# Second expert layer: the rank products of its second half put directly behind that half's router products, the shared expert's products put behind them, and products on zeros placed ahead of two waits

## The chip, the cores and the metric

The kernel runs on one core of one Trainium2 chip. Its time is that of one execution of the whole program in device microseconds (us), the median over several runs. TensorE (PE) has a granted clock with two levels here, 1.2 and 2.4 GHz; the profile prints it as a share of the higher one, so 0.50 is the lower level. VectorE is DVE, ScalarE is ACT, GpSimd is POOL, SyncE is SP.

## The reference

The input x has 4 batches of 256 tokens with 256 features, 1024 tokens in all. Four layers follow one another, each of the form x = x + tanh(gate) * layer(layernorm(x)): a sparse attention, an expert layer of 8 experts, a latent attention with 16 heads, and the second expert layer, in which the change lies. Cut to what matters here:

```python
    router_logits = (x @ gate_w).astype(jnp.float32)          # x: normed tokens, 1024 x 256; gate_w: 256 x 16
    scores = jax.nn.sigmoid(router_logits)
    _, selected = jax.lax.top_k(scores + expert_bias[None, :], K)      # K = 2 of E = 16 experts
    top_scores = jnp.take_along_axis(scores, selected, axis=1)
    top_scores = top_scores / (top_scores.sum(-1, keepdims=True) + 1e-20)
    shared = jax.nn.silu(x @ shared_gate_w) * (x @ shared_up_w) @ shared_down_w
    for e in range(E):
        gu = x @ experts_gate_up[e]
        g, u = jnp.split(gu, 2, axis=-1)
        routed = routed + comb[:, e:e + 1] * (jax.nn.silu(g) * u @ experts_down[e])
    return (shared + routed).reshape(b, s, h)
```

So each token has a shared expert, which needs no routing, and two of 16 experts that its router picks.

## The kernel before, in words

All tokens stay on the chip as 8 tiles of 128 tokens, worked on in two halves of 4 tiles (512 tokens). Each engine has an order of instructions of its own, written out by hand, and the engines wait for each other by semaphores. An engine works through its list strictly in that order.

The second expert layer starts when the last attention lap has been added to x. For each half (called 0 and 1, Python argument `hf`) the steps are these.

- DVE norms the tokens into `xn` (ACT norms two of half 1's four tiles, L368). PE transposes them (`pe_transpose`, L399), ACT copies the result in full precision (`plain1_act`, L544, into the tile named att_w_raw) and rounded (`act_high`, L409, xT_h), and DVE forms the rest (`low`, L415, xT_l).
- PE multiplies the router weights (`logits1_pe`, L554, 8 products of 16 columns). ACT takes the sigmoid (L561). DVE finds the two best experts per token (`choose1`, L568 to L581) and writes `chosen`, a 0/1 matrix of tokens by experts.
- PE counts, by products with a triangular matrix, how many earlier tokens picked the same expert (`rank_pe`, L591 to L599, small bf16 products into bank 2). The last of them raises the semaphore `s_rank`.
- DVE turns rank and choice into a row number, the slot (`slots`, L609 to L615), and raises `s_slot`.
- POOL writes each token's normed row into its two slots in DRAM (`Blocks.place`, L955), 8 indirect transfers (DMA_INDIRECT, destination `xn_slots`) for each half, each of one tile of 128 rows.

When all 16 transfers of both halves have landed and DVE has worked out which expert owns which block (`compact`, L621 to L627, and `owners`, L633 to L648, which raises `s_owner`), SP loads the blocks of 128 rows back (`moe_x`, L991). Then come 31 blocks, each with a transposition (L998), gate and up products (L1007), a transposition of the hidden rows (L1016) and a down product (L1023) on PE, and an indirect store to `y_rows` (L962) on POOL. At the end the two rows of a token are read back and added to x.

The shared expert runs between these steps: `ffn1.gateup` (L803) makes 12 products of 512 columns for each half: 8 with the rounded weights (`wt_h`: xT_h and xT_l, gate and up) and 4 with the weights' rest (`wt_l`). ACT applies silu (L740), DVE multiplies (L752), `pe_down_whole` (L825) makes the down products and DVE adds them to x (L776). The products of half 1 need xT_l of half 1, which DVE makes (L415) only behind `slots` of half 1.

`fill` (L1714) and `warm` (L1031) multiply zeros into a bank that nobody reads, 512 columns each. `warm` makes 15 of them when the third quarter of the scatters has landed and 8 when the fourth has; `FILLS` is 6.

## Time and profile before

| | before |
|---|---|
| median of 3 runs (lowest to highest) | 541.48 us (541.19 to 542.93) |
| the profiled execution, its own time | 542.32 us |
| its span, first to last instruction | 539.3 us |
| PE busy | 492.2 us (91%) |
| DVE busy | 413.0 us (77%) |
| mean granted PE clock over the span | 0.975 |

The profiled execution's own time is 3.0 us longer than its span: what lies around the first and the last instruction. A row of a timeline gives the start in the span, the busy time, engine, line, operation, output and inputs, shape and count, and in brackets how long the engine sat idle before it and what ended that. Durations of PE rows overlap, since products are pipelined and their ends are modelled: the pace of a series is read from starts.

### The profile page before, as it was taken

The page shows a single profiled execution, that of the slowest core. Times are in us where ns is not written, and L with a number is a line of the kernel's source. Part 1 is how long each engine was busy: PE and PEld are TensorE (multiplying, and loading weights), DVE is VectorE, ACT ScalarE, POOL GpSimd, SP SyncE. Part 2 cuts the span into 40 slices and gives each one's busy share as a digit, 9 for nine tenths or more (in the row PEclk, how much of TensorE's full clock was granted, in tenths as well). Part 3 has the DMA queues.
Part 4 walks back from the last instruction along what each step waited for, and adds up shares of the span by engine and source line. Part 5 has one row for each costly group of instructions (what it writes and reads, how often), then busy time and mean ns, then how long its engine had stood idle before and what let it go on. Part 6 is the DMA issues. An engine that isn't in the chain of part 4 may idle for free.

```text
span 539.3 us, 9166 instructions
## 1 busy us (share of the span) xinstructions
PE 492.2 (91%) x2781; PEld 380.6 (71%) x2781; DVE 413.0 (77%) x1054; ACT 310.6 (58%) x793; POOL 281.5 (52%) x291
## 2 busy tenths in 40 slices
PE   6976999989988997789999999999999977999986
PEld 3754688777867885457777777777776665778864
DVE  5998899974677759888999999999997864644322
ACT  4753654335554641377777777787776872155541
POOL 0060467657335733568787768786660026345560
PEclk9997999999999999999999999999999986999998
DMA  7596423223412319881909080816006502234416
GB/s 258 192 280 226 139 58 89 88 60 89 147 60 62 114 39 234 148 174 35 195 11 197 14 191 29 176 50 126 1 2 246 235 19 80 98 113 121 135 57 233
DMA packets 40281, 65.03 MB, mean 121 GB/s; under 512 B 4323, under 2 KB 30637, under 8 KB 39984
## 3 DMA queue, kind: packets, MB, share of 16 engines
q1 hardware_dynamic: 37984, 60.31, 40.7%
q0 software_dynamic: 2256, 4.21, 2.4%
q8 instruction: 20, 0.33, 0.3%
q14 instruction: 21, 0.17, 0.1%
HBM read 38.48 MB, written 27.99 MB: 123 GB/s over the span
## 4 chain that ended last, share of the span: by engine, by line
PE 62%; DVE 23%; issue 4%; DMA 3%; ACT 3%; POOL 2%; another core or an unknown queue 1%; SPq 1%; POOLq 0%; DVEq 0%
PE bank L1592 11%; PE bank L803 8%; PE bank L1647 5%; PE bank L1666 5%; PE bank L1636 5%; PE bank L1007 4%; PE bank L838 4%; PE bank L1609 3%; DVE left L1978 3%; PE bank L1626 3%; PE bank L1613 2%; PE bank L1627 2%; DVE best L1974 2%; PE bank L1023 2%; DVE hid L759 2%
## 5 line engine op out<-in xcount | busy, mean ns | idle before, releaser
L1424 POOL TENSOR_TENSOR qr<-qr 128x512 f32<-128x512 f32 x48 | 61.7, 1285 | 16.0 <-DVE qr L2090 16.0
L2090 DVE TENSOR_TENSOR qr<-bank,sinq 64x512 f32<-64x512 f32 x96 | 66.1, 689 | 2.2
L1825 ACT ACTIVATE silu<-bank,negm 128x256 f32<-128x256 f32 x128 | 59.3, 472 | 6.1 <-DVE negm L2104 6.0
L720 POOL TENSOR_TENSOR ffn_w_l<-ffn_raw,ffn_w_h 128x512 fp32r<-128x512 f32 x30 | 39.4, 1315 | 30.1 <-ACT ffn_w_h L732 30.0
L1429 POOL TENSOR_TENSOR hid<-silu,rden 128x256 f32<-128x256 f32 x55 | 33.8, 615 | 35.4 <-DVE rden L2109 35.3
L2104 DVE TENSOR_REDUCE negm<-bank 128x2 f32<-128x512 f32 x64 | 44.2, 691 | 6.3 <-PE bank L1627 3.7
L744 ACT ACTIVATE hid_h<-hid 128x512 fp32r<-128x512 f32 x28 | 17.7, 631 | 52.9 <-DVE hid L759 46.6
L1832 ACT ACTIVATE hid<-silu,rden 128x256 f32<-128x256 f32 x55 | 27.9, 507 | 34.2 <-DVE rden L2109 34.2
L962 POOL DMA_INDIRECT y_rows<-moe_y,route_rows x31 | 30.2, 974 | 31.1 <-issue 18.1
L1838 ACT ACTIVATE probsT<-bank 128x512 f32<-128x512 f32 x64 | 37.9, 592 | 9.8 <-PE bank L1636 9.6
L803 PE MATMUL bank<-xT_h,ffn_w_h 128*128 128x512 f32 x120 | 40.5, 419 | 2.9 <-DVE xT_l L415 2.9
L1636 PE MATMUL bank<-ident,hid 128*128 128x128 f32 x256 | 38.5, 273 | 2.4 <-POOL hid L1429 1.1
L803 PE MATMUL bank<-xT_l,ffn_w_h 128*128 128x512 f32 x120 | 39.4, 410 | 0.0
L1626 PE MATMUL bank<-ks_h,qs 128*128 128x256 f32 x128 | 34.6, 293 | 4.0 <-DVE qs L2098 2.5
L1592 PE MATMUL bank<-xT_h,att_w_h 128*128 128x512 f32 x96 | 34.5, 442 | 3.5 <-DVE xT_l L415 2.7
L803 PE MATMUL bank<-xT_h,ffn_w_l 128*128 128x512 f32 x120 | 34.1, 406 | 0.0
L2086 DVE TENSOR_TENSOR qr<-bank,cosq 128x512 f32<-128x512 f32 x48 | 32.7, 682 | 1.1 <-PE bank L1592 1.0
L1627 PE MATMUL bank<-ks_l,qs 128*128 128x256 f32 x128 | 32.8, 280 | 0.0
L740 ACT ACTIVATE silu<-bank 128x512 f32<-128x512 f32 x30 | 17.8, 593 | 26.0 <-PE bank L803 25.9
L838 PE MATMUL bank<-ffn_w_h,hid_h 128*128 128x256 f32 x112 | 28.5, 288 | 4.5 <-ACT hid_h L744 4.5
L1007 PE MATMUL bank<-moe_w,moe_xT 128*128 x124 | 32.1, 382 | 0.0
L1099 DVE COPY moe_hidT<-bank 128x128 f32<-128x128 f32 x31 | 9.0, 292 | 29.9 <-PE bank L1016 29.9
(259 smaller groups left out, 1393.2 us busy)
## 6 DMA issues: line engine op xcount, KB each, us to landing
xn_slots<-blank SPq DMA_DIRECT2D x8, 2056.0 KB, 12.9
ffn_raw<-in_w_ffn SPq DMA_DIRECT2D x30, 256.0 KB, 2.7
pair_w<-in_pair_w SPq DMA_DIRECT2D x8, 768.0 KB, 5.7
moe_w<-in_w_moe SPq DMA_DIRECT2D x1, 6144.0 KB, 18.2
moe_x<-xn_slots SPq DMA_DIRECT2D x31, 128.5 KB
ffn_raw<-in_w_ffn SPq DMA_DIRECT2D x30, 128.0 KB, 2.3
folds<-att_w_raw SPq DMA_DIRECT2D x6, 640.0 KB, 8.3
att_w_raw<-folds SPq DMA_DIRECT2D x6, 384.0 KB, 12.2
```

The lines of the kernel that those rows point to most:

```text
L720: nc.gpsimd.tensor_tensor(wt_l[b][:, 0:GU], raw[b][:, 0:GU], wt_h[b][:, 0:GU], ALU.subtract).then_inc(self.wgl, 1)
L803: last = nc.tensor.matmul(bank[self.up(st) + g][:], wp[st.b][:, (2 * kt + g) * P:(2 * kt + g + 1) * P], xp[:, kt, st.hf * 512:(st.hf + 1) ...
L838: last = nc.tensor.matmul(bank[4 + t // 2][:, (t % 2) * D:(t % 2 + 1) * D], hp[st.b][:, t * P:(t + 1) * P], wp[st.b][:, GU:WC], start=Fals ...
L1007: last = nc.tensor.matmul(bank[2 + b % 2][:, 0:2 * P], xgT[b % 2][:, k, :], cells[:, bass.ds(cell + k * 2 * P, 2 * P)], start=(k == 0), st ...
L1424: nc.gpsimd.tensor_tensor(qr[n][:, 0, :], qr[n][:, 0, :], qr[n][:, 1, :], ALU.add).then_inc(s_turned, 1)
L1592: last = nc.tensor.matmul(bank[bk][:], m_of(wp[w], k, j), xp[:, k, hf * 512:(hf + 1) * 512], start=(m == 0), stop=(m == 5))
L1626: nc.tensor.matmul(o, q, ks_h[:, keys], start=True, stop=False)
L1627: last = nc.tensor.matmul(o, q, ks_l[:, keys], start=False, stop=True)
L1636: last = nc.tensor.matmul(bank[6][:, (2 * h + k) * P:(2 * h + k + 1) * P], pn[u % 2][:, h, k * P:(k + 1) * P], ident[:], start=True, stop= ...
L1825: last = nc.scalar.activation(ex[u % 2][:, h, :], bank[4 + u % 2][:, h * S:(h + 1) * S], ACT.Exp, bias=negm[:, u % 2, h:h + 1], accum_out= ...
L2090: last = nc.vector.tensor_tensor(by_sin[other, :, :], q2[hs, :, :], sinq[hs, j:j + 1, :].broadcast_to([C, 2, S]), ALU.mult)
L2104: nc.vector.tensor_reduce(negm[:, u % 2, :], bank[4 + u % 2][:].rearrange("p (h n) -> p h n", h=2), AX_X, ALU.max, negate=True).then_inc(s ...
```

## The change

Only PE's order is touched, at one place behind the last attention lap. Eight products on zeros are put between the rank products of half 0 and the wait for half 1's normed tokens. Four more, and then the rank products of half 1, are put directly behind half 1's router products. The first half's shared expert products, which in the kernel before enclose the rank products of half 1 (8 ahead of them, 4 behind), come behind them as one series of 12. The wait on `s_slot` (half 0's ranks read from bank 2) moves with the rank products.

```diff
                 logits1_pe(pe, 0)
                 fill(FILLS, 5)
                 rank_pe(pe, 0)
+                fill(8, 5)
                 n_ffn1[1].pe_transpose(pe)
                 logits1_pe(pe, 1)
+                pe.wait_ge(s_slot, 1)
+                fill(4, 5)
+                rank_pe(pe, 1)
                 n_ffn1[0].pe_whole(pe)
-                ffn1.gateup(pe, ffn1_first, ((wt_h, (0, 1)),))
-                pe.wait_ge(s_slot, 1)
-                rank_pe(pe, 1)
-                ffn1.gateup(pe, ffn1_first, ((wt_l, (0, 1)),))
+                ffn1.gateup(pe, ffn1_first)
                 n_ffn1[1].pe_whole(pe)
                 ffn1.gateup(pe, ffn1_second)
```

On PE, from half 0's last rank products (L599) on, the rows of the change with + and those of before with - read as follows; bank<-zero is a product on zeros, ident,xn the transposition, rg_raw,att_w_raw the router products.

```order
 L599 MATMUL bank<-chosen,route_tri 128x32
 L599 MATMUL bank<-chosen,route_tri 128x16
+L1714 MATMUL bank<-zero 128x512 x8
 L399 MATMUL bank<-ident,xn 128x128 x8
 L554 MATMUL bank<-rg_raw,att_w_raw 128x16 x8
-L803 MATMUL bank<-xT_h,ffn_w_h 128x512 x2
-L803 MATMUL bank<-xT_l,ffn_w_h 128x512 x2
-L803 MATMUL bank<-xT_h,ffn_w_h 128x512 x2
-L803 MATMUL bank<-xT_l,ffn_w_h 128x512 x2
+L1714 MATMUL bank<-zero 128x512 x4
 L591 MATMUL bank<-route_expert_rows,route_tri 128x64
 L593 MATMUL bank<-chosen,route_tri 128x64
```

Eight shared expert products have left the place between the router products and the rank products, and zeros stand in two places.

Behind half 1's last rank products, the same engine goes on like this; ffn_w_h are the rounded weights of the shared expert, ffn_w_l their rest.

```order
 L599 MATMUL bank<-chosen,route_tri 128x32
 L599 MATMUL bank<-chosen,route_tri 128x16
+L803 MATMUL bank<-xT_h,ffn_w_h 128x512 x2
+L803 MATMUL bank<-xT_l,ffn_w_h 128x512 x2
+L803 MATMUL bank<-xT_h,ffn_w_h 128x512 x2
+L803 MATMUL bank<-xT_l,ffn_w_h 128x512 x2
 L803 MATMUL bank<-xT_h,ffn_w_l 128x512 x4
 L803 MATMUL bank<-xT_h,ffn_w_h 128x512 x2
```

The eight products that left stand here now, so that 12 products of the first half follow the rank products, where 4 did. The order of DVE, ACT, POOL and SP is the same in both kernels.

## Rows read from the trace of the kernel before

**Rows 1.** The page: the span.

```profile
span 539.3 us, 9166 instructions
```

**Rows 2.** The chain that ended last, 448 to 470 us: start, us, what.

```profile
448.37 4.67 another core or an unknown queue
...
463.70 3.14 DMA xn_slots<-moe_xn_second,route_slot_at
...
467.59 2.17 DMA moe_x<-xn_slots
```

**Rows 3.** Timeline of POOL, its indirect transfers.

```profile
450.76 0.98 POOL L955 DMA_INDIRECT xn_slots<-moe_xn_second,route_slot_at  x1 [0.30 <-issue]
454.74 0.97 POOL L955 DMA_INDIRECT xn_slots<-xn,route_slot_at  x1 [3.00 <-DVE route_slot_at L615]
```

**Rows 4.** Timeline of DVE: half 1's choice and slots, the owners' first and last instruction.

```profile
448.33 0.23 DVE L581 TENSOR_TENSOR chosen<-one_hots 128x64 bf16<-128x64 f32 x1
453.06 0.29 DVE L609 TENSOR_TENSOR route_smul<-one_hots,bank 128x128 f32<-128x128 f32 x1 [4.50 <-remote]
...
453.70 0.17 DVE L615 CAST route_slot_at<-route_slot 128x8 uint32<-128x8 f32 x1
...
461.00 0.15 DVE L633 TENSOR_TENSOR route_ends<-route_base,route_nblk 1x16 f32<-1x16 f32 x1
...
464.77 0.17 DVE L648 COPY route_owner<-route_row_f 1x31 f32<-1x31 f32 x1
```

**Rows 5.** Timeline of PE around the change, and its first block's transposition.

```profile
433.63 1.85 PE L554 MATMUL bank<-rg_raw,att_w_raw 128*128 128x16 f32 x16
435.33 1.63 PE L1714 MATMUL bank<-zero 128*128 128x512 f32 x6
...
441.23 1.38 PE L399 MATMUL bank<-ident,xn 128*128 128x128 f32 x8 [2.16 <-DVE xn L374]
442.66 3.57 PE L554 MATMUL bank<-rg_raw,att_w_raw 128*128 128x16 f32 x16
...
449.63 0.28 PE L591 MATMUL bank<-route_expert_rows,route_tri 128*128 128x64 bf16 x1
...
450.02 0.34 PE L599 MATMUL bank<-chosen,route_tri 128*128 128x64 bf16 x4
450.21 2.05 PE L803 MATMUL bank<-xT_h,ffn_w_l 128*128 128x512 f32 x4
455.12 0.88 PE L803 MATMUL bank<-xT_h,ffn_w_h 128*128 128x512 f32 x2 [2.86 <-DVE xT_l L415]
...
459.57 3.62 PE L825 MATMUL bank<-ffn_raw,hid 128*128 128x256 f32 x16
462.83 3.80 PE L1031 MATMUL bank<-zero 128*128 128x512 f32 x15
466.88 2.14 PE L1031 MATMUL bank<-zero 128*128 128x512 f32 x8 [0.25 <-DMA xn_slots<-moe_xn_second,route_slot_at]
469.07 0.44 PE L998 MATMUL bank<-ident,moe_x 128*128 128x128 f32 x2
```

**Rows 6.** Timeline of ACT: half 1's sigmoid, and the shared expert's silu.

```profile
446.26 0.23 ACT L561 ACTIVATE sc<-bank 128x64 f32<-128x64 f32 x1 [1.99 <-PE bank L554]
...
453.12 0.60 ACT L740 ACTIVATE silu<-bank 128x512 f32<-128x512 f32 x1 [4.35 <-PE bank L803]
459.77 0.60 ACT L740 ACTIVATE silu<-bank 128x512 f32<-128x512 f32 x1 [6.05 <-PE bank L803]
```

**Rows 7.** Stretches: length, busy us by engine, PE clock, DMA share, GB/s.

```profile
436.00:442.60 6.60, 2.63 (x18) 1.62 (x16) 5.92 (x35) 5.49 (x10) 1.01 (x1) 0.95 0.00 0
442.60:452.20 9.60, 9.54 (x39) 7.62 (x38) 1.90 (x16) 4.12 (x7) 7.01 (x8) 0.50 0.28 98
...
455.10:460.00 4.90, 4.88 (x15) 3.88 (x16) 1.98 (x5) 0.23 (x1) 3.68 (x5) 0.65 0.23 81
...
470.00:480.00 10.00, 9.74 (x54) 7.87 (x54) 4.00 (x19) 5.42 (x17) 2.92 (x3) 1.00 0.28 83
```

## The prediction

> **What bounds the kernel now.** I read the chain of waits first, then the timelines of the engines that it names, then the stretches with the clock. Between 448 and 470 us the chain holds 4.67 us in which DVE waits for a source that the view can't name, later 3.14 us from the last scatter's start to its landing, and 2.17 us for a load of moe_x [rows 2]. The unnamed wait is DVE's first `slots` instruction of half 1 (L609, 4.50 us idle), and in the code it waits for s_rank alone [rows 4]. POOL is the next link: its eight scatters of half 0 end at 450.76 + 0.98 = 451.74, then it sits idle 3.00 us until the slots of half 1 are there, and starts their scatters at 454.74 [rows 3]. Each follows the last after 0.30 us, so the other seven, the landing, the loads and the blocks all hang on that start. From there to the end the chain has no link that was ready long before. So a time that POOL's second series gains is gained whole, if nothing else is late, and the most that it can gain here is 454.74 - (451.74 + 0.30) = 2.70 us.
>
> Why are the slots late? PE makes half 1's router products from 442.66 on in 3.57 us; the same series of half 0 took 1.85 [rows 5]. The granted clock says why: 0.50 from 442.6 to 452.2, after 0.95 in the 6.6 us ahead, in which PE was busy 2.63 us [rows 7]. That is the 1.2 GHz level. Sigmoid at 446.26, chosen written at 448.33 + 0.23 = 448.56 [rows 4, 6]. PE is then still in its eight shared expert products, and starts the rank products 1.07 us later, at 449.63; their last row ends at 450.02 + 0.34 = 450.36 [rows 5]. DVE starts only at 453.06, 2.70 us after that end. ACT's silu, which waits for the four products behind (they end at 450.21 + 2.05 = 452.26), starts at 453.12, 0.86 us after [rows 5, 6]. Two signals with 1.9 us of work between them arrive nearly together. The second silu started 459.77, without such a lag. So 2.7 us of the delay is a late signal whose cause these views don't show; it is the main unknown below.
>
> **The change part by part.** *Eight zeros behind half 0's rank products.* PE is idle 2.16 us before its transpositions at 441.23, so from 439.07 [rows 5]. Six zeros take 1.63 us at full clock and 15 take 3.80, so one more costs 2.17 / 9 = 0.24 us, and eight cost 1.63 + 2 x 0.24 = 2.1: they end by 441.2. Cost nothing while the clock is full, as it is until about 441.9 (0.95 of 6.6 us leaves 0.66 us at half). At the lower level they would take twice that, and the transpositions would start 2.2 us later, at 443.4. The cover is then the slack that follows below.
>
> *Four zeros behind half 1's router products.* At most 1.1 us (1.63 x 4 / 6), or 2.2 at half clock. `chosen` comes 448.56 - 446.26 = 2.30 us after the sigmoid's start, so they are hidden in either case.
>
> *Rank products ahead of the shared expert's.* They no longer wait out eight products. They start when `chosen` is there. They took 450.36 - 449.63 = 0.73 us at half clock.
>
> *The clock.* If the zeros keep PE at 2.4 GHz, the router products take 1.85 and not 3.57 us, and everything behind is 1.72 us earlier. I work out both.
>
> Half clock: chosen 448.56, rank products to 449.3, slots (453.06 to 453.87 before, 0.81) done at 450.1. Full clock: chosen at 446.84, ranks at most to 447.6, slots done at 448.4. POOL needed 454.74 - 453.87 = 0.87 us from the slots to its first scatter, so slots at 452.04 - 0.87 = 451.17 are early enough. Both cases meet it, with 1.1 and 2.8 us to spare, and POOL then goes from its eighth scatter straight to the ninth at 452.04. **The gain is 2.70 us in both**: it does not hang on the clock, and it takes in most of a late signal at full clock (2.70 late makes slots at 451.1, just enough) but not at half clock (452.8, so a start at 453.7 and a gain of 1.1).
>
> *Twelve shared expert products behind.* They start at 447.6 or 449.3. A product of 512 columns costs 0.24 us, as a zero does, and 0.48 at half clock (four took 2.05 there [rows 5]), so twelve end at 450.5 or 455.1. Half 1's twelve need xT_l, which DVE makes in some 1.3 us behind `slots`, and end at 453.4 or, half clock all the way, 460.9. Then the down products, 3.62: done at 457.0 or 464.5, before at 463.2 [rows 5]. The owners took 464.94 - 461.00 = 3.94 us [rows 4] behind half 1's hidden rows; these now come 1.3 us (silu and product) behind the end of its twelve, so owners end at 458.6 or at worst 466.1. SP needs them with the last landing, at 463.70 + 3.14 - 2.70 = 464.14. Only half clock from 442 to 460 without a break would break this, by 2 us; before, the clock was half for about 10 us and then again for (1 - 0.65) x 2 x 4.9 = 3.4 us [rows 7], so I take it as covered.
>
> *Zeros of `warm`.* 15 of them wait for the third quarter of the scatters. They now start at about 459.6 and take 3.8; the last eight start when the last quarter has landed, 464.1, take 2.14, and end at 466.3 [rows 5]. The first block's transposition would start at 469.07 - 2.70 = 466.37. Just covered at full clock; at half clock they end at 468.4 and cost 2.0.
>
> **The sum.** For the profiled execution 542.32 - 2.70 = 539.62 us, a span of 539.3 - 2.7 = 536.6 [rows 1]. Its own time was 0.84 above the median of the runs; from the median, 541.48 - 2.70 = 538.8 us. That is the forecast, 0.5% faster. A difference of 0.3% (1.6 us) is about what a measurement of this kernel can tell from no change.
>
> **The rivals.** *The signal of the rank products waits for the products behind it.* For it: the two signals that came together, 0.7 to 0.9 us behind the end of the series. Against it: the router products' signal, also followed by a series at once, was out by 446.26, 0.03 after their last row's end (442.66 + 3.57) [rows 5, 6]. If it holds, the ranks are now followed by twelve products and not by four. The signal then comes 0.7 behind their end, at 451.2 or 455.8; slots 0.81 and POOL 0.87 later make 452.9 or 457.5 against 454.74. The time goes from 1.8 us faster to 2.8 slower, with the clock: 539.7 to 544.3, and in the middle 542.0. The Trainium skill bears on it (Perfetto Trace Analysis, Tensor Engine Instruction): a matmul's end in the profile is an estimate, and its signal leaves only when PSUM has acknowledged the writes. By it 450.36 need not be the true end, but it names nothing that ties a signal to later products. The trace doesn't decide.
>
> *The late signal belongs to that one traced execution.* Without it the slots were ready at about 451.2 and POOL hardly waited. Then the gain is about 0.2: 541.3. For it: nothing else in the trace is late like this. Against it: this execution was only 0.84 us above the median, so at most about a third of the 2.7 can be its own, unless the profile saved time elsewhere.
>
> *PE's clock falls in the blocks: slower.* PE has now a gap of 2.6 us between the down products (457.0) and the zeros at 459.6, and one of about 0.7 ahead of 464.1. Before it had only 0.25 us in that place [rows 5], and the clock stood at 1.00 from 460 to 480 [rows 7]. In the stage behind, PE is busy 9.74 of 10 us, so a stretch at half clock loses up to half its length. A stretch of 3.4 us costs 1.7 and leaves 1.0: 540.5. One of about 10 us, as at 442, costs 5.1, so 543.9, slower. From 2 x 2.70 = 5.4 us at half the change turns to a loss, from 8.6 to one that can be measured. Against it: after the zeros at 435.33 PE idled some 1.8 us and the clock stayed full. The Trainium skill speaks against this change here (TensorE: Matmul & The Clock Gate, Why this matters for your kernels): it tells to leave no long idle gap between bursts of products, or the clock goes back to half. The trace agrees at 442 (2.63 busy of 6.6 us, then 0.50).
>
> **How the numbers follow.** Gain of 2.7 us whole or nearly so (538.8; own range 538.2 to 539.8): 0.52. Signal tied to the series behind: 0.22, of it 0.07 faster, 0.11 within 0.3%, 0.04 slower. Lateness of the traced execution alone: 0.13, no difference. Clock falls in the blocks: 0.13, of it 0.09 within 0.3% and 0.04 slower. Faster 0.59, same 0.33, slower 0.08. The range from 538.2 to 542.0 leaves out the long half-clock stretch and the worst of the tied signal on one side, and on the other a little for landings that turn out quicker.
>
> **What the profile would show.** POOL's ninth scatter 0.30 us behind the eighth, near 452.0, and no idle row there; DVE's L609 near 447.6 (full clock) or 449.4 (half); the router products of half 1 in about 1.9 us if the zeros hold the clock. moe_x loads from 464.4 on, the first L998 near 466.4, the span 536.6. If L609 starts behind the end of the L803 series instead, the first rival is right. A clock under 1.00 in the 10 us behind the first L998 is the third. What would make me wrong outright: a new wait on s_owner at SP, or the block stage taking longer than its 70 us before (469.07 to 539.3).

## The result, and the profile after

The changed kernel takes 549.94 us (median of 4 executions, 548.25 to 551.66), the kernel before 541.51 us beside it. The ratio is 1.013, 95% interval [1.0103, 1.0157]: slower, where 538.8 us were forecast, and outside the range up to 542.0. A ratio here and below is the record's own estimate, which leaves out three disturbed executions of 696 to 2216 us and need not equal the quotient of the medians (here 1.0156). The profiled execution took 551.42 us.

The page's span, to be held against [rows 1], is 10.3 us longer:

```profile
span 549.6 us, 9189 instructions
```

POOL's timeline (start, us, line, what, and in brackets the idle time before it) shows at the eighth and ninth scatter that the announced step took place:

```profile
451.98 0.97 POOL L955 DMA_INDIRECT xn_slots<-moe_xn_second,route_slot_at  x1 [0.30 <-issue]
453.25 0.97 POOL L955 DMA_INDIRECT xn_slots<-xn,route_slot_at  x1 [0.30 <-issue]
...
462.20 0.97 POOL L955 DMA_INDIRECT xn_slots<-moe_xn_second,route_slot_at  x1 [0.30 <-issue]
```

The 3.00 us of idle time in [rows 3] are gone, and the last scatter starts at 462.20 instead of 463.70, although this execution entered the stage 1.24 us later (the transpositions of half 0 start at 432.00, before at 430.76). POOL has gained its 2.7 us. The end did not, and PE's timeline says where to look:

```profile
440.16 3.14 PE L1714 MATMUL bank<-zero 128*128 128x512 f32 x8
443.10 1.62 PE L399 MATMUL bank<-ident,xn 128*128 128x128 f32 x8
444.94 1.93 PE L554 MATMUL bank<-rg_raw,att_w_raw 128*128 128x16 f32 x16 [0.21 <-ACT att_w_raw L544]
446.71 1.18 PE L1714 MATMUL bank<-zero 128*128 128x512 f32 x4
...
449.46 0.25 PE L599 MATMUL bank<-chosen,route_tri 128*128 128x64 bf16 x4
...
451.52 1.09 PE L803 MATMUL bank<-xT_h,ffn_w_l 128*128 128x512 f32 x4
453.55 0.73 PE L803 MATMUL bank<-xT_h,ffn_w_h 128*128 128x512 f32 x2 [0.93 <-DVE xT_l L415]
...
455.52 1.09 PE L803 MATMUL bank<-xT_h,ffn_w_l 128*128 128x512 f32 x4
465.75 6.60 PE L825 MATMUL bank<-ffn_raw,hid 128*128 128x256 f32 x16 [9.13 <-DVE hid L752]
472.00 5.60 PE L1031 MATMUL bank<-zero 128*128 128x512 f32 x23
477.43 0.60 PE L998 MATMUL bank<-ident,moe_x 128*128 128x128 f32 x4
```

The shared expert's two series end at 452.61 and 456.61. Then PE stands idle for 9.13 us, which [rows 5] don't have, for `hid`. The down products take 6.60 us (3.62 before), all 23 zeros of `warm` come behind them, and the first block starts at 477.43 instead of 469.07. Why is `hid` late? ACT's timeline:

```profile
446.90 0.22 ACT L561 ACTIVATE sc<-bank 128x64 f32<-128x64 f32 x1 [0.51 <-issue]
...
464.31 0.60 ACT L740 ACTIVATE silu<-bank 128x512 f32<-128x512 f32 x1 [14.90 <-remote]
465.82 0.60 ACT L740 ACTIVATE silu<-bank 128x512 f32<-128x512 f32 x1 [0.91 <-remote]
```

ACT has nothing queued ahead of silu and waits for PE's products alone. It sees them 11.7 us (464.31 - 452.61) and 9.2 us (465.82 - 456.61) after their recorded ends, and POOL's last scatter ended at 462.20 + 0.97 = 463.17, 1.1 us before the first. In [rows 6] ACT started 0.86 us behind the products. DVE's timeline has the same ailment in small, and what follows from it:

```profile
451.49 0.29 DVE L609 TENSOR_TENSOR route_smul<-one_hots,bank 128x128 f32<-128x128 f32 x1 [2.29 <-remote]
...
465.00 0.69 DVE L752 TENSOR_TENSOR hid<-silu,bank 128x512 f32<-128x512 f32 x1 [10.07 <-issue]
...
467.05 0.15 DVE L633 TENSOR_TENSOR route_ends<-route_base,route_nblk 1x16 f32<-1x16 f32 x1
...
470.81 0.17 DVE L648 COPY route_owner<-route_row_f 1x31 f32<-1x31 f32 x1
```

The rank products end at 449.71 and `slots` begins 1.78 us later (2.70 before, [rows 4]). The owners, behind `hid` on DVE, end at 470.98 and no longer at 464.94, so SP's loads start at 471.84, long after the last landing. Signals of other engines are prompt in the same microseconds: `xT_l` ends on DVE at 453.49 and PE goes on at 453.55.

The chain of waits (start, us, what) names 10.01 us of it "issue", which is what that view prints where it finds no releaser; it is the late signal:

```profile
454.93 10.01 issue
465.00 0.70 DVE hid L752
465.75 6.60 PE bank L825 x16
472.35 5.25 PE bank L1031 x23
```

Some stretches of the windows (length, busy us of PE, PEld, DVE, ACT and POOL, PE's granted clock, DMA share, GB/s) give the clock:

```profile
436.00:442.60 6.60, 4.80 (x25) 3.73 (x25) 6.12 (x37) 5.35 (x10) 0.00 (x0) 0.87 0.00 0
...
450.00:460.00 10.00, 5.69 (x24) 3.95 (x22) 3.27 (x9) 0.00 (x0) 7.56 (x9) 1.00 0.27 98
460.00:470.00 10.00, 4.25 (x10) 3.46 (x11) 4.10 (x8) 1.19 (x2) 2.56 (x3) 0.57 0.13 48
470.00:480.00 10.00, 9.67 (x43) 7.82 (x43) 5.36 (x18) 1.13 (x4) 0.00 (x0) 0.92 0.18 53
```

After the idle stretch PE is back at 1.2 GHz: 0.57 from 460 to 470, where before it was 1.00. Of the 10.3 us, 8.4 lie ahead of the first block, and of these 1.24 are this execution's later entry, so the stage itself takes 7.1 us more. The blocks to the end take 2.0 us more than before (549.6 - 477.43 = 72.2 against 70.2); in the kept traces in which the down products stay ahead of the blocks, that part varied from 68.7 (e6) to 74.4 us (e8, e14), and I draw nothing from it.

### The profile page after: what moved, and what is told of

Same layout as the page of the kernel before. It is cut to its first block, busy times and chain, and to the rows that moved or that the text cites. A ratio compares the mean times of both kernels' runs of the same rounds, so it can differ in the third digit from the quotient of the medians.

```text
span 549.6 us, 9189 instructions
## 1 busy us (share of the span) xinstructions
PE 496.2 (90%) x2793; PEld 382.9 (70%) x2793; DVE 412.8 (75%) x1054; ACT 310.6 (57%) x793; POOL 281.1 (51%) x291
## 4 chain that ended last, share of the span: by engine, by line
PE 59%; DVE 24%; issue 5%; DMA 4%; ACT 4%; POOL 1%; SPq 1%; another core or an unknown queue 0%; POOLq 0%; DVEq 0%
PE bank L1592 10%; PE bank L803 8%; PE bank L1647 5%; PE bank L1666 5%; PE bank L1636 5%; PE bank L1007 3%; PE bank L838 3%; PE bank L1609 3%; DVE left L1979 3%; PE bank L1626 2%; PE bank L1627 2%; PE bank L1613 2%; DVE best L1975 2%; DVE hid L759 2%; DVE silu L757 2%
## 5 line engine op out<-in xcount | busy, mean ns | idle before, releaser
L803 PE MATMUL bank<-xT_h,ffn_w_h 128*128 128x512 f32 x120 | 39.0, 406 | 0.9 <-DVE xT_l L415 0.9
L803 PE MATMUL bank<-xT_l,ffn_w_h 128*128 128x512 f32 x120 | 37.7, 394 | 0.0
L740 ACT ACTIVATE silu<-bank 128x512 f32<-128x512 f32 x30 | 17.8, 593 | 31.4 <-remote 15.8
L803 PE MATMUL bank<-xT_h,ffn_w_l 128*128 128x512 f32 x120 | 32.8, 395 | 0.0
```

The source lines that it names most:

```text
L803: last = nc.tensor.matmul(bank[self.up(st) + g][:], wp[st.b][:, (2 * kt + g) * P:(2 * kt + g + 1) * P], xp[:, kt, st.hf * 512:(st.hf + 1) ...
```

## The experiments

The kernels ran in five batches, each beside the kernel before; a label names one kernel, and the text shortens it to e1, e2 and so on. The expectations name theories by letters. In words, the main ones are: an unbroken series of indirect transfers on POOL holds back PE's signals, in the strictest form until it ends (A); the zeros cause it (B); it belongs to single executions (C); both order and zeros are needed (F); the lateness grows with the number of PE's instructions (G); what holds the signals is POOL's issuing of indirect transfers and not their traffic (I).

| batch | kernel | median us | before us | ratio, 95% interval |
|---|---|---|---|---|
| 1 | e1_no_zeros | 540.37 | 538.92 | 1.003 [0.9995, 1.0065] |
| 1 | e2_pool_pause | 546.92 | 538.92 | 1.017 [1.0012, 1.0329] |
| 1 | e3_before_eight | 539.65 | 538.92 | 1.0006 [0.997, 1.0043] |
| 1 | e4_owners_first | 541.33 | 538.92 | 1.0068 [1.0039, 1.0097] |
| 2 | e5_change_again | 548.23 | 542.26 | 1.0108 [1.0077, 1.014] |
| 2 | e6_before_again | 542.08 | 542.26 | 0.9998 [0.9979, 1.0017] |
| 2 | e7_only_four | 549.52 | 542.26 | 1.0136 [1.0102, 1.0171] |
| 2 | e8_only_eight | 548.09 | 542.26 | 1.0107 [1.0068, 1.0145] |
| 3 | e9_no_zeros_2 | 547.74 | 542.12 | 1.01 [1.0054, 1.0146] |
| 3 | e10_pool_pause_2 | 545.45 | 542.12 | 1.0064 [1.0043, 1.0086] |
| 3 | e11_owners_first_2 | 550.63 | 542.12 | 1.0155 [1.011, 1.02] |
| 3 | e12_few_products | 542.02 | 542.12 | 0.9996 [0.9975, 1.0018] |
| 4 | e13_narrow | 549.01 | 541.97 | 1.0124 [1.0072, 1.0177] |
| 4 | e14_plain_in_pause | 555.11 | 541.97 | 1.0237 [1.0178, 1.0296] |
| 4 | e15_no_warm | 548.58 | 541.97 | 1.0111 [1.0071, 1.0151] |
| 4 | e16_before_eight_2 | 547.16 | 541.97 | 1.0108 [1.0048, 1.0169] |
| 5 | e17_order_late_downs | 541.36 | 539.31 | 1.0035 [1.0017, 1.0053] |
| 5 | e18_before_late_downs | 540.79 | 539.31 | 1.0031 [1.0017, 1.0045] |

### Batch 1: the zeros, the pause, the owners

e1_no_zeros is the change without either group of zeros.

```diff
                 rank_pe(pe, 0)
-                fill(8, 5)
                 n_ffn1[1].pe_transpose(pe)
...
                 pe.wait_ge(s_slot, 1)
-                fill(4, 5)
                 rank_pe(pe, 1)
```

> The change without either series of zeros: only the order of the rank products and the shared expert's products is changed. In the changed kernel both silu instructions start at 464.3 and 465.8 us, 11.7 and 9.2 us behind the recorded end of their products, and the owners follow them. Theory A (PE's signals are held back while POOL's scatters run on without a pause): POOL's two series still join here, so silu again starts near 464 and the time is about 550. Theory B (the zeros cause it, by filling PE's queue or by the clock): without them silu starts within 1 us of its products and the time is about 539.

e2_pool_pause is the change with a pause on POOL ahead of half 1's scatters, until PE has signalled both shared expert series.

```diff
+                if hf:
+                    pool.wait_ge(ffn1.gu, 2)
```

> The changed kernel with one wait more: POOL starts half 1's scatters only when both halves' gate and up products have signalled. Theory A: with POOL at rest from 453 us on, the two signals arrive near 454 and 457 us, scatters start near 458 instead of 453.3, the last lands near 470, and the time is about 545 (5 us of scatters later than in the changed kernel, but no 10 us wait for the owners). Theory B: the signals stay late, about 10 us behind their products, and the scatters start near 465 only: about 553 or more.

e3_before_eight is the kernel before with the eight zeros alone (`fill(8, 5)` at the same place).

> The kernel before with the eight zeros alone. Theory A: POOL still pauses between the series, because the rank products stay behind the eight shared expert products; signals come in that pause, and the time is within 1.5 us of before. Theory B: signals late, time 545 or more.

e4_owners_first is the change with `owners` ahead of the hidden rows on DVE.

```diff
                 compact(dve, seq)
+                owners(seq)
                 ffn1.hidden(dve, ffn1_first)
                 ffn1.hidden(dve, ffn1_second)
-                owners(seq)
```

> The changed kernel with DVE's owners ahead of its two hidden products. If the loss comes only by way of s_owner, which sits behind the late silu on DVE, SP can load the blocks when the last scatter has landed (464.3) and 541 to 545 comes out, the rest being the down products that end late (near 472). If the signals' lateness itself moves, the silu start tells so. Both theories leave the silu late here, since neither POOL's order nor the zeros change.

The three without a pause came out within 2 us of one another, and in none of the four traces is a signal late. ACT's timeline of e1_no_zeros:

```profile
454.82 0.60 ACT L740 ACTIVATE silu<-bank 128x512 f32<-128x512 f32 x1 [4.82 <-PE bank L803]
457.62 0.60 ACT L740 ACTIVATE silu<-bank 128x512 f32<-128x512 f32 x1 [2.20 <-PE bank L803]
```

and PE's, with the last products of the two series:

```profile
453.69 1.09 PE L803 MATMUL bank<-xT_h,ffn_w_l 128*128 128x512 f32 x4
456.49 1.09 PE L803 MATMUL bank<-xT_h,ffn_w_l 128*128 128x512 f32 x4
```

The products end at 454.78 and 457.58 and silu starts 0.04 us later, while POOL's scatters run on unbroken to 463.4. So theory A in its strict form, that every signal waits for the end of an unbroken series, does not hold always; and because nothing was late, zeros, pause and owners' place could not be judged here. The kernel before was itself 2.6 us faster than in the first comparison (538.92 against 541.51). I had to repeat with the change itself in the batch.

### Batch 2: change and before again, and each group of zeros alone

e5_change_again and e6_before_again are the two kernels unchanged. e7_only_four is the change without the eight zeros, e8_only_eight the change without the four (one of the two lines removed above in each).

> The changed kernel itself, unchanged, once more. In its first trace PE's signals came up to 11.7 us late; in the last four kernels, one of which has the same order on PE, none was late. Theory C (the lateness is something that an execution or a chip has or has not, and not a property of this order): signals prompt, half 1's scatters 0.30 us behind half 0's, first block near 466.3, the time within 1.5 us of the kernel before on this chip. Theory D (this very program brings it on): silu near 464 again and a time 7 to 9 us above before.

> The kernel before, unchanged, for a trace on the same chip as the others. Theory C: half 1's rank signal prompt (it was 2.70 us late in the first trace), slots near 451.3, POOL hardly pausing between its series, first block near 466.5. Theory D, and my prediction's main case: the signal again 2.7 us late, scatters of half 1 at 454.7, first block at 469.

> The change with the four zeros ahead of the rank products and without the eight ahead of the transpositions. If the eight zeros cost by a clock that falls while they run (8 zeros took 3.1 us in the changed kernel and pushed the transpositions 1.9 us back), this one has its transpositions at once and is 0 to 1.5 us faster than the changed kernel. If the zeros' place does not matter, no difference.

> The change with the eight zeros and without the four. The four are covered by the wait for the chosen experts, so no difference to the changed kernel beyond 0.5 us is expected; a clear gain would say that they fill PE's queue and cost there.

The slowdown is back in all three changed kernels, with either group of zeros. It is the same mechanism: silu starts 464.11 in e7_only_four for products that end at 455.55, in e5_change_again the first series is 1.6 us late and the second 7.3 (455.86, seen at 463.18), and in e8_only_eight 1.7 and 6.0. All six executions of e5 took 546 us or more. So C falls. The traced e6_before_again repeats the late rank signal of the kernel before, seen on DVE and POOL:

```profile
454.23 0.29 DVE L609 TENSOR_TENSOR route_smul<-one_hots,bank 128x128 f32<-128x128 f32 x1 [3.94 <-remote]
```

```profile
452.05 0.98 POOL L955 DMA_INDIRECT xn_slots<-moe_xn_second,route_slot_at  x1 [0.30 <-issue]
455.91 0.97 POOL L955 DMA_INDIRECT xn_slots<-xn,route_slot_at  x1 [2.89 <-DVE route_slot_at L615]
```

Its rank products end at 451.79, so the signal is 2.4 us late and makes POOL pause. Behind the pause the second shared expert series ends at 461.70 and silu starts at 461.74: prompt, while POOL is issuing again since 455.91.

### Batch 3: the first questions again, and fewer products

e9_no_zeros_2, e10_pool_pause_2 and e11_owners_first_2 repeat e1, e2 and e4. e12_few_products makes 4 products for each half of the shared expert in place of 12; it leaves out the weights' rest and the part of xT_l.

```diff
                 n_ffn1[0].pe_whole(pe)
-                ffn1.gateup(pe, ffn1_first)
+                few(ffn1_first)
                 n_ffn1[1].pe_whole(pe)
-                ffn1.gateup(pe, ffn1_second)
+                few(ffn1_second)
```

> The change without its zeros, once more, since the first time its chip showed no late signal in any kernel. Theory E (a chip either delays PE's signals or not; where it does, they come about 1 us after POOL's scatter series ends, if the series has run some 8 us): on a chip that delays, the order alone is enough: POOL's series join or nearly so, silu near 463 and a time 5 to 8 us above before. Theory F (the zeros' additional instructions are needed for it): signals within 2.5 us and a time within 2 us of before. On a chip that doesn't delay, about 1.4 us above before, as the first time.

> The changed kernel with POOL's second series behind the shared expert's signals, once more. Theory E on a chip that delays: signals about 1 us after the first series ends (near 454), hence 4 to 6 us above before, and not more than on a chip that does not delay (8 us at the median there). If the signals need something else than POOL's rest, they come 10 us late here too and the time is 12 us or more above before.

> The changed kernel with the owners ahead of the hidden products on DVE, once more. On a chip that delays: silu late again (near 463 to 464), owners done near 455; PE must still make the down products and 23 zeros behind them (to about 475), so the time is 3 to 5 us above before and 2 to 4 us below the changed kernel (6 to 8 above before). On a chip that doesn't: 2.4 above before, as the first time.

> The changed kernel with 4 instead of 12 shared expert products in each half (those of the weights' rest and of xT_l are left out, so the shared expert is computed coarsely). Theory G (PE's signals queue up behind a backlog that PE's own instructions make, which drains while the scatters run): with 16 products fewer the signals come many microseconds earlier than 464, and the time is within 2 us of before. Theory E (they wait for the scatter series to end, whatever PE did): silu near 463 all the same, and 5 to 8 us above before.

Without zeros the change is about as slow as with them (1.01, where e5 had 1.0108). ACT's timeline of e9_no_zeros_2, whose products end at 455.74 and 458.55:

```profile
462.92 0.60 ACT L740 ACTIVATE silu<-bank 128x512 f32<-128x512 f32 x1 [12.31 <-remote]
465.80 0.60 ACT L740 ACTIVATE silu<-bank 128x512 f32<-128x512 f32 x1 [2.28 <-remote]
```

So B and F fall, the order does it alone. With the pause the signals are prompt. ACT's and POOL's timelines of e10_pool_pause_2 (its L957 is the change's L955):

```profile
454.96 0.60 ACT L740 ACTIVATE silu<-bank 128x512 f32<-128x512 f32 x1 [5.97 <-PE bank L803]
457.34 0.60 ACT L740 ACTIVATE silu<-bank 128x512 f32<-128x512 f32 x1 [1.78 <-PE bank L803]
```

```profile
452.60 0.97 POOL L957 DMA_INDIRECT xn_slots<-moe_xn_second,route_slot_at  x1 [0.30 <-issue]
458.11 0.97 POOL L957 DMA_INDIRECT xn_slots<-xn,route_slot_at  x1 [4.54 <-PE bank L803]
```

The products end at 454.52 and 457.30 and are seen 0.44 and 0.04 us later, where the joined series made it 7 to 12 in the first comparison and in e7, e9 and e11, and in e5 and e8 only 1.6 and 1.7 for the first signal and 6 to 7 for the second. The pause costs its own 4.54 us, so the last scatter starts at 467.06 and the first block at 473.26, and the kernel ends at 1.0064: it takes back 2.3 us of the 5.6 that e9 lost in the same batch, or 2.6 of the 6.0 of e5, and still loses to before, whose pause is 3 us.

e11_owners_first_2 tells who holds the end. It was expected 3 to 5 us above before and came 8.5 above (550.63 against 542.12). Its owners are done at 457.30 and SP loads from 465.38 on, as forecast without late signals; the down products still wait for `hid`, run from 465.39 to 471.95, the 23 zeros follow, and the first block starts at 477.05. The owners' place gives nothing back, since PE is as late on its own.

In e12_few_products the two series end at 450.31 and 452.58 and are seen 2.2 and 3.5 us later, at 452.48 and 456.06. The time is that of before (0.9996), but it leaves out two thirds of these products, so that both series also end earlier within POOL's (8.0 and 10.2 us behind its first scatter, against 11.2 and 14.0 in e5). Its down products end at 460.67 and DVE sees them only when the scatters are over:

```profile
465.30 2.73 DVE L776 SCALAR_TENSOR_TENSOR x<-bank,tg,x 128x512 f32<-128x512 f32 x4 [3.75 <-remote]
```

### Batch 4: columns or instructions, issue or traffic

e13_narrow keeps the number of products and cuts each from 512 to 64 columns; it leaves out 448 of 512 tokens of each half in the shared gate and up products.

```diff
-                ffn1.gateup(pe, ffn1_first)
+                narrow(ffn1_first)
...
+                                        bank[ffn1.up(st) + g][:, 0:64], wp[st.b][:, (2 * kt + g) * P:(2 * kt + g + 1) * P],
+                                        xp[:, kt, st.hf * 512:st.hf * 512 + 64],
```

> The changed kernel with the same 24 shared expert products and their weight loads, but each 64 columns wide and not 512 (448 of 512 tokens of each half are left out of the shared expert's gate and up). Where the kernel before takes about 542 us (a batch with late signals): theory G1 (the delay follows the number of PE's instructions) - silu of half 0 and 1 come as late as in the changed kernel, 6 us or more behind the products, 547 or more. Theory G2 (it follows the streamed columns, what is written to the banks) - the lateness is under 2 us, as with 4 products a half, and the time within 2 us of before.

e14_plain_in_pause is e10 with 20 plain transfers issued by SP, from the scatters' sources to a spare buffer. In the trace SP issues them from 449.45 to 459.71, so that they begin before the pause (452.56 to 457.18) and outlast it.

```diff
+                if hf:
+                    pool.wait_ge(ffn1.gu, 2)
...
+                for c in range(20):
+                    sp.dma_start(plain[c * P:(c + 1) * P, :],
+                                 (xn_id, xb)[c % 2][:, c // 2 % 4, :]).then_inc(s_trigk, 16)
+                sp.wait_ge(s_trigk, 16 * 21)
```

> The changed kernel with POOL's second series behind the shared expert's signals (the pause of the earlier kernel), and in the pause 20 plain transfers of the same tiles from SP to a spare tensor. Theory H (the transfers' traffic holds PE's signals): the two silu come only when the plain transfers have landed, 5 us or more late, and the time is 550 or more. Theory I (what POOL does to issue indirect transfers holds them): signals within 0.5 us of their products as in the plain pause, and 545 to 547.

e15_no_warm is e11 without any zeros, those of `warm` included (`self.warm(pe)` removed too).

> The change without its zeros, with the owners ahead of the hidden products on DVE, and without the 23 zeros of warm. If the time lost by the late signals goes by way of PE's own list (down products, then 23 zeros, then the first block), the first block starts 4 to 5 us earlier than without this (475.1 there), near 470.5, and the time is 0 to 2 us above before. If it is lost otherwise, it stays 5 us above.

e16_before_eight_2 repeats e3.

> The kernel before with the eight zeros alone, once more. In a batch with late signals: they let the clock stay full, so half 1's ranks come early and POOL's series join although the order is that of before. If joined series and a backlog bring the delay (theory G), this kernel is 3 to 6 us above before; if the order of the rank products is needed, within 1.5 us.

ACT's timeline of e13_narrow, and the last products of PE's two series:

```profile
457.49 0.60 ACT L740 ACTIVATE silu<-bank 128x512 f32<-128x512 f32 x1 [9.50 <-remote]
465.29 0.60 ACT L740 ACTIVATE silu<-bank 128x512 f32<-128x512 f32 x1 [7.21 <-remote]
```

```profile
450.08 1.04 PE L1732 MATMUL bank<-xT_h,ffn_w_l 128*128 128x64 f32 x4
...
452.64 1.04 PE L1732 MATMUL bank<-xT_h,ffn_w_l 128*128 128x64 f32 x4
```

The ends are 451.12 and 453.68, so the signals are 6.4 and 11.6 us late with an eighth of the columns, against 2.2 and 3.5 in e12 with a third of the products. So what the products stream does not matter. That their number does is what these two kernels suggest, but they are one trace each, and the signals of the unchanged order of products differ as much between traces (1.6 us in e5, 11.7 in the first comparison). The times speak for it too: all eight executions of e12 took 543.65 us or less, both of e13 548.18 or more.

In e14_plain_in_pause the signals stay prompt with the plain transfers going on (L741 is L740 here):

```profile
454.03 0.60 ACT L741 ACTIVATE silu<-bank 128x512 f32<-128x512 f32 x1 [6.04 <-PE bank L804]
456.41 0.60 ACT L741 ACTIVATE silu<-bank 128x512 f32<-128x512 f32 x1 [1.78 <-PE bank L804]
```

```profile
449.45 0.33 SPq L1397 DMA_DIRECT2D plain_rows<-xn  x1
...
459.27 0.44 SPq L1397 DMA_DIRECT2D plain_rows<-moe_xn_second  x1
```

The products end at 453.58 and 456.38: 0.45 and 0.03 us. So plain traffic of SP does not hold them; whether it is POOL's issuing of indirect transfers or the packets of those transfers, no run separates. The kernel's time I had missed: 555.11 us, because the scatters now land late behind the plain transfers, and the chain of waits holds

```profile
461.00 12.22 DMA xn_slots<-moe_xn_second,route_slot_at
```

for the landing of the second series' fourth scatter, on which the zeros of `warm` wait. The chain of e10_pool_pause_2 has 3.05 us for the same one:

```profile
461.94 3.05 DMA xn_slots<-moe_xn_second,route_slot_at
```

That says nothing on the signals.

e15_no_warm was expected 0 to 2 us above before and came 6.6 above (548.58 against 541.97). Against the change it brought nothing that I can tell (548.23 and 549.94 in two other batches). Its signals were late like the others' (458.74, seen at about 466), PE idled 8.65 us, the downs ran to 473.35, mostly at half clock (5.96 us), DVE's sums came behind them, and the first block started at 475.63 at half clock. The zeros of `warm` had stood on the path of the change with 5.25 us; without them other late work stood there.

e16_before_eight_2 came out 5.2 us slower than before at the median (547.16), but its four executions are 541.20, 544.89, 549.43 and 550.11, so the median says little, and the traced one is the fastest. That trace shows the pattern of before, with a rank signal 2.7 us late (448.92, seen at 451.61) and a pause on POOL of 1.64 us. What the other three look like I didn't see. If the pause is short or absent there, the cause is the same; that is argued and not shown.

### Batch 5: taking the late work off the path

e17_order_late_downs is the new order without zeros, owners first, and with the shared expert's down products and sums behind the 31 blocks. e18_before_late_downs is the kernel before with the same three moves.

```diff
                 ffn1.gateup(pe, ffn1_second)
+                blocks.prog_pe(pe)
                 ffn1.pe_down_whole(pe, ffn1_first)
                 ffn1.pe_down_whole(pe, ffn1_second)
-                pe.wait_ge(ffn1.hid, 2)
-                blocks.prog_pe(pe)
+                pe.wait_ge(ffn1.acc, 2)
```

On DVE the hidden products and the work of the blocks go ahead of the sums in the same way.

> The change without its zeros (it was 5.6 us above before in a batch with late signals), with the owners ahead of the hidden products on DVE, and the shared expert's down products and sums behind the 31 blocks, where PE waits for POOL's last stores. The cost theory (late signals cost because down products and sums lie between them and the first block): silu still late, 463 to 466, but the first block at 467.5 and not 475, and 1 to 3 us faster than before. If the late signals reach the blocks in another way (silu and copies in ACT's order, the clock), it stays 2 us or more above before.

> The kernel before with the same three moves and the order of the rank products as before. There the first block follows the loads by 2.0 us already, so the down products are not on the path: within 1.5 us of before. A gain like the other kernel's would say that moving the down products gains by itself.

Both are slower than before by 0.3% (1.0035 and 1.0031), and in both traces no signal was late: e17's series end at 454.10 and 456.90 and silu starts at 454.14 and 456.94. It was a batch like the first (before 539.31). So it does not decide whether moving the downs pays when signals are late, and no version here beats the kernel before.

## Why the prediction was wrong

**What held.** The unnamed wait of DVE was a late rank signal (again in e6), and POOL's idle time hung on it. The new order removed the idle time to the last hundredth: the ninth scatter follows the eighth in 1.27 us. Neither group of zeros is needed for the loss (e9). The shared expert's two series ended 2.1 and 3.2 us after the 450.5 and 453.4 worked out, of which 1.2 is this execution's later entry.

**The step that failed.** "2.7 us of the delay is a late signal whose cause these views don't show" was right, and behind it I priced the lateness as a fixed thing: 2.70 us, or in the first rival 0.7 us behind the series that follows. I then let the hidden rows come "1.3 us (silu and product) behind the end of its twelve", owners at 458.6, at worst 466.1. That is the term that failed: the signals of the two series of twelve came 11.7 and 9.2 us late, half 1's hidden rows were done at 467.14, 10.5 us behind the end of their twelve, and the owners ended at 470.98. The announced case "a new wait on s_owner at SP" came about, but it was not what held the first block: SP's loads began at 471.84, and PE was in its down products and 23 zeros until 477.43 (11.68 us from 465.75 on). For these the sum had nothing, since it had the downs done by 464.5 at worst and the zeros by 466.3, or 468.4 at half clock. The 464.5 was too early on its own terms: it is the case of half clock all the way, and takes the down products at their full clock price of 3.62 us; at the 6.60 measured mostly at the lower level it is 467.5. "Only half clock from 442 to 460 without a break would break this" was taken as the single danger to the owners; the clock was full from 450 to 460 and the signals were late all the same.

**The mechanism in its place.** From the two kernels and the experiments of batches 2 to 4: PE's signals are seen late while POOL issues indirect transfers without a break. The table gives traces of those batches and the first comparison; "into the series" is the time from the first scatter of the unbroken series to the recorded end of the products. These are reads of timelines like those above.

| kernel | series began | end, seen | into the series | late |
|---|---|---|---|---|
| e5, ranks | 441.83 | 447.89, 447.93 | 6.1 | 0.04 |
| after, ranks | 442.83 | 449.71, 451.49 | 6.9 | 1.8 |
| before, ranks | 441.59 | 450.36, 453.06 | 8.8 | 2.7 |
| after, first twelve | 442.83 | 452.61, 464.31 | 9.8 | 11.7 |
| e5, first twelve | 441.83 | 453.06, 454.70 | 11.2 | 1.6 |
| e5, second twelve | 441.83 | 455.86, 463.18 | 14.0 | 7.3 |
| e12, first four | 442.34 | 450.31, 452.48 | 8.0 | 2.2 |
| e13, second twelve narrow | 442.44 | 453.68, 465.29 | 11.2 | 11.6 |
| e6, second twelve, after the pause | 455.91 | 461.70, 461.74 | 5.8 | 0.04 |
| e10, second twelve, in the pause | none | 457.30, 457.34 | - | 0.04 |

Up to 6.1 us into a series no rank or silu signal is late in these batches. From 6.9 us on most are, by amounts that differ from execution to execution; a pause resets it. What PE did just before counts as well, and the rank signals show it best: with the eight shared expert products directly ahead of the rank products they are 2.4 to 2.7 us late (before, e6, e16; 7.4 to 8.9 us into the series), without these eight and 7.2 to 8.2 us into the series only 0.04 to 0.4 (e7, e9, e11, e15); the 1.8 of the first comparison is the exception. And of the 14 silu signals that came 6 us or more late, 11 were seen 0.9 to 3.0 us behind the end of the last scatter, as the 464.31 above; three were seen before that end (e13 457.49, e8 462.54, e9 462.92). The kernel before breaks its 16 scatters in two series of 8 with 3 us between them, and each of its two groups of PE's long products is seen in the break or within 5.0 us (5.8 in e6) of the next series' start. The change made one series of 16, 20 us long, with all 24 products inside it. The pause that I counted as 2.7 us of loss was what let the signals through. Shown are: in such a batch the order alone does it (e9), a pause makes the signals prompt (e10), plain transfers on SP's queue don't bring it back (e14), and it needs no wide products (e13). That the number of products counts is supported by e12 and by the rank signals, and not isolated. That it builds up like a backlog is the reading that fits these; no run varied the length of a series alone.

The page Perfetto Trace Analysis of the Trainium skill (Tensor Engine Instruction) says that a product's end in the profile is worked out, and that the signal goes out when PSUM has acknowledged the writes. This case's trace agrees that recorded end and signal are two things (452.61 and 464.31), but nothing on the page leads to a gap of 11.7 us, and with no POOL series, as in e10, it was 0.04 to 0.44.

**The path from there to 8 us.** The late signals idle PE for 9.13 us; the clock falls, and the down products cost 6.60 us and not 3.62. Here the Trainium skill's advice against long idle gaps between bursts (TensorE: Matmul & The Clock Gate, Why this matters for your kernels) agrees with the trace (0.57 from 460 to 470). Down products from 465.75 on, with 6.60 us of their own and 5.25 of zeros behind them, as the chain above has them, make 477.6, near the first block's 477.43, where 469.07 stood. e11 and e15 show that owners and zeros are no separate levers: take one away and the next late thing stands in its place.

**The eight zeros.** "They end by 441.2. Cost nothing while the clock is full": the clock fell at about 440.9 in this execution, one microsecond sooner than before and, counted from the stage's start (432.00 and 430.76), 2.3 us sooner, amid the zeros (0.87 over 6.6 us is 1.7 us at the lower level, up to 442.6). They took 3.14 us in place of 2.1, and the transpositions began at 443.10, about 0.6 us later than the 441.23 + 1.24 at which their input came. So the zeros did not hold the clock here: it is 0.50 in PE's windows from 441 to 444. But it was back at about 444.3 (0.85 from 444 to 445, then 1.00), ahead of the router products, which ran in 1.93 us and not 3.57. Of the other traces with these zeros, e2, e11 and e16 have them at 3.15 to 3.32 us, the rest at about 2.07; and in all twelve traces with them the router products took 1.93, in all eight without them 3.57. Neither mattered for the end.

**The rivals.** The first (a signal tied to what follows) pointed at PE's signals but had the mechanism wrong: the rank signal was seen at 451.49, 1.1 us before the twelve products behind it ended at 452.61, and the second twelve, with nothing issued behind them, were 9.2 us late. Even at its worst it ended at 544.3. The second, that the lateness belongs to the traced execution alone, was wrong as put, but batches 1 and 5 show its substance: there are batches in which no signal is late, the kernel before takes 538.9 and 539.3 us, about 2.5 us less, its two series join there by themselves (e18, which has its order on PE up to there and no added zeros, has the eighth scatter at 450.98 and the ninth at 452.26; the kernel before itself left no trace in these batches), and the new order has nothing to win (e1 1.003, e4 1.0068). So the forecast gain existed only where late signals existed, and those made it a loss. The third (clock falls in the blocks) didn't come: the granted clock is 1.00 from 477.4 to 520, as these rows of the changed kernel's windows show:

```profile
477.40:487.40 10.00, 8.82 (x48) 6.84 (x47) 2.75 (x15) 4.75 (x15) 1.94 (x2) 1.00 0.23 62
487.40:500.00 12.60, 12.60 (x72) 10.63 (x71) 7.38 (x31) 7.07 (x24) 7.32 (x8) 1.00 0.44 126
500.00:520.00 20.00, 18.65 (x103) 15.25 (x102) 6.14 (x35) 10.86 (x35) 11.58 (x13) 1.00 0.46 127
```

**What stays open.** What in the chip holds the signals, and whether it is the signals or the products themselves that run behind their records, whose ends are modelled; whether the issuing on POOL or the packets of the indirect transfers matter; why some batches are free of it (batches 1 and 3 ran on one chip, 4 and 5 on another, so the chip is not it); why equal series give 1.6 us in one trace and 11.7 in another; whether recording the traces has a part in it, since all the times here come from recorded executions; and what late down products would bring when signals are late, as batch 5 had none.

## What to carry to other kernels

Before you remove an idle stretch, ask what drains in it: here a stretch of 3 us in which POOL did nothing let the signals of another engine through, and closing it cost 6 to 8 us in the batches with late signals. A delay that no view can name must not enter a sum as a constant; treat it as something that may grow with load, and price what hangs on the same engine's next signals, above all where you move more work behind them. And repeat both kernels in several batches before judging a difference below 1%: here the kernel before itself moved by 0.6% between batches, and a single batch would have cleared the change of blame.

## What the runs showed of the hardware that was not expected

- PE's signals reached ACT and DVE up to 11.7 us after the recorded end of the products while POOL issued indirect transfers one after another (0.97 us each, 0.30 us apart). In the same stretch DVE's signal to PE took 0.06 us, and ACT's silu to DVE's `hid` 0.09 (464.91 to 465.00).
- The lateness did not need wide products (12 of 64 columns: 6.4 and 11.6 us; 4 of 512 columns: 2.2 and 3.5, one trace each) and was gone in a POOL pause of 4.5 us (at most 0.45), with plain transfers of SP going on too. Rank signals 7.2 to 8.9 us into a series were 2.4 to 2.7 us late with eight long products just ahead of them and mostly at most 0.4 without.
- 20 plain transfers of 128 rows, issued by SP before and beside eight scatters, made the landing of the fourth of these 12.22 us in the chain (e14), against 3.05 without them (e10).
- PE's fall to half clock in the same gap came 11.2 us behind the stage's start in one execution and 8.9 in another (441.9 - 430.76, 440.9 - 432.00), so eight zeros placed to end "before it" took 3.14 us instead of 2.1.
